# Down products of the feed-forwards: stationary split weights with 512 moving tokens, in place of stationary tokens with 128 moving columns

## The chip, the cores and the metric

The kernel runs on one core of one Trainium2 chip. The metric is the device time of one execution in microseconds. The kernel before took 3348.98 us (median of three runs, 3345.56 to 3355.31).

## The reference

4096 tokens (8 chunks of 512) of width 128 go through six stages, each preceded by a layer norm and added back to x: a gated mixture of experts (F0a), a banded attention (A0), the same mixture again (F0b), a second mixture (F1a), an attention by hyperbolic distance (A1), and that second mixture again (F1b). Only the four feed-forwards are changed. What they compute:

```python
# F0a, F0b: two shared and eight routed feed-forwards, hidden width 256
_ffn = silu(x @ w1.T) * (x @ w3.T) @ w2.T
x = x + 0.5 * (sum over e of cw[t, e] * _ffn_e(norm(x)) + sum of the two shared ones)
# F1a, F1b: eight routed ones, hidden width 512; cw is 0 where an expert's capacity is passed
h = square(relu(norm(x) @ c_fc[e]))
x = x + 0.5 * sum over e of cw[t, e] * (h @ c_proj[e])
```

cw holds two non-zero weights for each token (a softmax over its two best logits). Both kernels compute every expert for every token and weigh the results.

## The kernel before, in words

Tokens are handled in chunks of 512. XT holds the normed tokens transposed (128 features on the partitions, tokens along the row), X the running sum with tokens on the partitions. Each feed-forward phase (ffn_phase) first runs the routing (route_vector and its partners) as a program block of its own and then, after all engines have met, a loop over the 8 chunks.

The up products use float32r operands, split into a high part and a rest: xs holds the chunk's tokens as hi and lo (split_gpsimd, L199 and L201), up_hi and up_lo the weights. For each block j of 128 hidden units (20 of them in F0, 32 in F1) TensorE makes w_lo*x_hi + w_hi*x_lo + w_hi*x_hi (L221 to L223), each with 128x128 stationary weights and 512 moving tokens; in F0 a block has two such groups, w1 and w3. ScalarE takes Silu or Relu out of PSUM (L257), VectorE multiplies by the w3 product or by itself (L282). The down products (L231) are plain float32: the stationary side is 128 tokens of hT, the moving side 128 columns of dn, so that each hidden block costs four products, and each product is two instructions in the trace. They lie one expert behind the up products. VectorE then multiplies each expert's output by its routing weight and adds it up (L290), four instructions of 128x128 per expert, the last of them into X. While chunk c runs, the norm of chunk c-1 is worked in at fixed experts e (stats at 0, apply at 2, turn at 3, logits at 5 and 6). In F1 the up weights are loaded at the start of the phase and split by ScalarE (L658) and GpSimd (L644).

Order is fixed by the code of each engine and by semaphores; nothing is scheduled automatically. Banks: four for the up products in rotation, two for the down products.

Of the kernel before, what the change touches and what calls it, by code (L numbers as in the profile page):

```python
# [13 lines left out]
P = 128  # L14
# [5 lines left out]
E = 8  # L20
# [14 lines left out]
def macaron(nc, x, alpha, w_qkv0, bias_rows0, wo0, wo0_t, wfc0, router0, expert_bias, up0, down0,  # L35
            w_qkv1, wo1, router1, up1, down1, out, stop_after=99):
    ctx = ExitStack()
    with ctx:
# [21 lines left out]
        cw = sb("cw", [P, TILES, E])  # L60
        cw_c = sb("cw_c", [P, TPC, E])
# [12 lines left out]
        staged_free = sem("staged_free")  # L74
# [7 lines left out]
        for n in names:  # L82
            kinds = ["tr_done", "xt_copied", "lg_done", "lg_copied", "var_ready", "rstd_ready", "xn_ready"]
            if n == "P":
                kinds.append("split_done")
            if n[0] == "F":
                kinds += ["xs_free", "split_done", "up_done", "act_done", "h_ready", "dn_done", "acc_done"]
# [114 lines left out]

        def ffn_tensor(eng, s, lay, XS, hT, w_hi, w_lo, dn, nxt):
            U, HB, G, RING = ffn_shape(lay)
            free = s["h_ready"] if lay == 0 else s["act_done"]
            norm_credits_tensor(eng, s)
            eng.sem_inc(s["dn_done"], 2)
            eng.sem_inc(s["xs_free"], 2)
            with eng.Fori(0, B) as c:
                eng.wait_ge(s["split_done"], c + 1)  # L210
                xh = XS[:, bass.ds((c % 2) * 2 * S, S)]
                xl = XS[:, bass.ds((c % 2) * 2 * S + S, S)]
                for e in range(U + 1):
                    if e < U:
                        for hb in range(HB):
                            j = e * HB + hb
                            eng.wait_ge(free, c * (U * HB) + j + 1)
                            for g in range(G):
                                bank = (j * G + g) % 4
                                cols = slice((hb * G + g) * P, (hb * G + g + 1) * P)  # L220
                                eng.matmul(ps[:, bank, :], w_lo[:, e, cols], xh, start=True, stop=False)  # L221
                                eng.matmul(ps[:, bank, :], w_hi[:, e, cols], xl, start=False, stop=False)  # L222
                                last = eng.matmul(ps[:, bank, :], w_hi[:, e, cols], xh, start=False, stop=True)  # L223
                            last.then_inc(s["up_done"], 1)
                    if e > 0:
# [1588 lines left out]
```

## Time and profile before

| | |
|---|---|
| median of 3 runs | 3348.98 us |
| profiled execution | 3349.0 us, span 3347.2 us |
| mean granted TensorE clock | 0.861 of full speed |
| F0a, first up product to last accumulation | 63.5 to 435.7 us |
| F0b | 965.2 to 1344.8 us |
| F1a | 1380.1 to 1790.5 us |
| F1b | 2933.4 to 3339.9 us |

Busy shares over the whole span are TensorE 83%, VectorE 67%, ScalarE 56%, GpSimd 26%. They mix stages that differ: in the four feed-forwards TensorE is busy nearly all the time at the full clock, in A1 (1791 to 2925 us) the granted clock is 0.67. So the stages are read one by one: busy times by stretch, then the timeline of one engine inside a stretch, then the list of who waited for whom.

### The profile page before, as it was taken

What the parts mean: (1) busy time and instruction counts of PE and PEld (TensorE: products, weight loads), DVE (VectorE), ACT (ScalarE), POOL (GpSimd) and SP (SyncE); (2) the same over time, 40 slices, a digit from 0 to 9 for tenths busy, and PEclk for the clock granted to TensorE, in tenths of its full rate; (3) what the DMA queues carried; (4) which work ended last, traced back from release to release, by engine and by line L of the source; (5) the groups of instructions that cost most, each with busy time, mean ns of one, the idle gap of its engine ahead of it and who ended that gap; (6) DMA issues with size and microseconds to landing.
All of it is one profiled execution on the core that took longest, in us unless ns stands there. A gap on an engine that the chain in (4) does not pass through costs nothing. (4 is left out here: it accounts for less than half of the span.)

```text
span 3347.2 us, 52294 instructions
## 1 busy us (share of the span) xinstructions
PE 2792.1 (83%) x17860; PEld 2081.7 (62%) x17862; DVE 2227.0 (67%) x5046; ACT 1886.0 (56%) x2052; POOL 875.3 (26%) x584
## 2 busy tenths in 40 slices
PE   4999968888869999699996687787787787399998
PEld 4888856666658888599995232332232332189998
DVE  5555557777745555666666787787877878456665
ACT  2222237677712222334431999999999999433333
POOL 1000010000000000100001657666766767300000
PEclk9999979999979999799997667667666766699999
DMA  2000000000000000100000000000000000100000
GB/s 82 0 0 0 0 1 2 0 0 0 0 1 0 0 0 0 51 0 0 0 0 0 0 0 0 1 1 1 1 1 0 0 0 0 50 1 0 0 0 25
DMA packets 3224, 18.43 MB, mean 6 GB/s; under 512 B 1088, under 2 KB 2112, under 8 KB 2112
## 3 DMA queue, kind: packets, MB, share of 16 engines
q1 hardware_dynamic: 3136, 17.32, 1.3%
q8 instruction: 48, 0.79, 0.1%
q14 instruction: 40, 0.33, 0.0%
HBM read 15.22 MB, written 2.10 MB: 5 GB/s over the span
## 5 line engine op out<-in xcount | busy, mean ns | idle before, releaser
L1402 POOL TENSOR_TENSOR A_Y<-A_Y,A_U 128x2048 f32<-128x2048 f32 x86 | 389.8, 4554 | 227.7 <-ACT A_U L1445 227.7
L1478 DVE TENSOR_SCALAR A_U<-ps 128x1024 f32<-128x1024 f32 x256 | 309.2, 1218 | 125.6 <-POOL A_Y L1402 64.7
L140 POOL TENSOR_TENSOR rstd<-var_eps,half_neg 128x4 f32<-128x4 f32 x45 | 49.7, 1105 | 1208.0 <-DVE var_eps L120 1183.1
L1484 DVE SCALAR_TENSOR_TENSOR A_U<-ps,A_U 128x1024 f32<-128x1024 f32 x256 | 311.2, 1216 | 58.8 <-PE ps L1614 58.8
L1614 PE MATMUL ps<-A_QT,A_KT 9*128 9x512 f32 x512 | 182.9, 711 | 195.5 <-DVE A_U L1484 162.6
L257 ACT ACTIVATE F1b_act<-ps 128x512 f32<-128x512 f32 x256 | 153.2, 598 | 247.4 <-PE ps L223 231.2
L257 ACT ACTIVATE F1a_act<-ps 128x512 f32<-128x512 f32 x256 | 153.2, 598 | 243.2 <-PE ps L223 226.8
L1614 PEld LDWEIGHTS ps<-A_QT,A_KT 9*128 9x128 f32 x512 | 66.6, 256 | 333.7 <-DVE A_U L1484 235.8
L257 ACT ACTIVATE F0b_act<-ps 128x512 f32<-128x512 f32 x160 | 95.6, 598 | 273.5 <-PE ps L223 273.5
L257 ACT ACTIVATE F0a_act<-ps 128x512 f32<-128x512 f32 x160 | 95.6, 598 | 266.2 <-PE ps L223 266.2
L231 PEld LDWEIGHTS ps<-dn,F1b_hT 128*128 128x128 f32 x2048 | 237.2, 192 | 4.4
L231 PEld LDWEIGHTS ps<-dn,F1a_hT 128*128 128x128 f32 x2048 | 237.2, 192 | 4.4
L231 PE MATMUL ps<-dn,F1a_hT 128*128 128x128 f32 x2048 | 237.6, 275 | 0.0
L231 PE MATMUL ps<-dn,F1b_hT 128*128 128x128 f32 x2048 | 237.6, 275 | 0.0
L1445 ACT ACTIVATE A_U<-A_U 128x2048 f32<-128x2048 f32 (+1 forms) x96 | 236.5, 2464 | 0.0
L1586 PE MATMUL ps<-A_Y,A_VA 128*32 128x512 f32 x688 | 228.7, 798 | 5.8 <-DVE A_OT L1384 3.0
L841 ACT ACTIVATE A_M<-A_M,A_nmax 128x192 f32<-128x192 f32 (+1 forms) x512 | 203.9, 471 | 35.4 <-DVE A_nmax L956 34.1
L1402 POOL TENSOR_TENSOR dn<-dn,A_U 128x2048 f32<-128x2048 f32 x42 | 190.7, 4563 | 114.2 <-ACT A_U L1445 114.2
L956 DVE CUSTOM_DVE_ANT_0 A_M<-ps,A_mask 128x192 f32<-128x192 f32 (+1 forms) x512 | 169.2, 387 | 46.8 <-PE ps L1007 46.0
L1603 PE MATMUL ps<-A_QT,A_KT 28*128 28x512 f32 x512 | 168.3, 675 | 37.3 <-DVE A_U L1478 32.9
L282 DVE TENSOR_TENSOR F0b_hT<-F0b_act,ps 128x512 f32<-128x512 f32 x160 | 109.4, 688 | 119.1 <-ACT F0b_act L257 118.0
L1444 ACT ACTIVATE A_Y<-A_U 128x2048 f32<-128x2048 f32 (+1 forms) x64 | 159.3, 2489 | 50.8 <-DVE A_U L1484 50.6
(336 smaller groups left out, 6635.5 us busy)
## 6 DMA issues: line engine op xcount, KB each, us to landing
dn<-in_down SPq DMA_DIRECT2D x2, 2048.0 KB, 12.5
stage<-in_up SPq DMA_DIRECT2D x1, 2560.0 KB, 9.3
X<-in_x SPq DMA_DIRECT2D x1, 2048.0 KB, 7.9
F1a_up<-in_up SPq DMA_DIRECT2D x1, 2048.0 KB, 7.9
F1b_up<-in_up SPq DMA_DIRECT2D x1, 2048.0 KB, 8.1
out_x<-X SPq DMA_DIRECT2D x1, 2048.0 KB, 6.3
dn<-in_down SPq DMA_DIRECT2D x1, 1280.0 KB, 11.9
qkv_w_s<-in_w_qkv SPq DMA_DIRECT2D x2, 192.0 KB
```

Source lines behind the costliest of these rows:

```text
L231: last = eng.matmul(ps[:, 4 + d % 2, t * P:(t + 1) * P], hT[:, d % 2, hb, t * P:(t + 1) * P], dn[:, d, hb, :], start=(hb == 0), stop=(hb = ...
L257: eng.activation(act_out[:, j % RING, :], ps[:, (j * G) % 4, :], ACT.Silu if lay == 0 else ACT.Relu).then_inc(s["act_done"], 1)
L841: last = eng.activation(m, m, ACT.Exp, scale=-1.0, bias=nmax[:, n % MR, b, r:r + 1])
L956: last = eng.tensor_tensor_reduce(M[:, n % MR, b, r, w0:w1], ps[:, 2 * (n % 2) + b, r * WIN + w0:r * WIN + w1], mask[:, w0:w1], -1.0, 3e38 ...
L1402: eng.tensor_tensor(flat(y_slot(m, h)), flat(y_slot(m, h)), flat(Um[:, h % UR]), ALU.add).then_inc(s["t_ready"], 1)
L1444: eng.activation(y, u, ACT.Sqrt, bias=1.0)
L1445: eng.activation(u, u, ACT.Sqrt).then_inc(s["s_ready"], 2 if joined else 1)
L1478: eng.tensor_scalar(u_step(n), d_pair(n), 0.0, None, ALU.max).then_inc(s["dp_vector"], 1)
L1484: eng.scalar_tensor_tensor(out=u, in0=g_pair(), scalar=CLAMP, in1=u, op0=ALU.min, op1=ALU.mult).then_inc(s["u_ready"], 1)
L1586: last = eng.matmul(ps[j:j + 32, OUT, :], VA[:, v0:v0 + 32], y_slot(m, h)[:, kt, :], start=(kt == 0), stop=(kt == TPC - 1))
L1603: last = eng.matmul(ps[:, 2 * (n % 2) + b, :], KT[r:r + 28, pair, kt * P:(kt + 1) * P], QT[r:r + 28, pair, :], start=True, stop=True)
L1614: last = eng.matmul(ps[:, 4 + b, :], KT[r:r + 9, pair, kt * P:(kt + 1) * P], QT[r:r + 9, pair, :], start=True, stop=True)
```

## The change

The down product is turned round. The stationary side is now a 128x128 block of the down weights, split into dn_hi and dn_lo at the start of each phase (ScalarE L908, GpSimd L933), and the moving side is 512 tokens of the hidden activation, split into hi and lo (tile hl). Three float32r products per hidden block (L268 to L270) add into one PSUM bank over all blocks of all experts, so the chunk's output comes out once, transposed; ScalarE copies it out (yT), TensorE turns it back with four transposes, and VectorE adds it to X in one instruction. Since experts are now summed in PSUM, the routing weight must enter before the product. It is laid out along the row, broadcast to all partitions: the routing result cw is transposed on TensorE, copied by ScalarE (as a square root in F1, since the weighed value is squared afterwards), written to DRAM, and read back for each chunk in two halves of 1 MB (weights_sync) into cwb.

In F0 GpSimd multiplies the product of each routed block by cwb, ScalarE makes hi by a copy, VectorE makes lo by a subtraction. In F1 VectorE does relu times cwb in one instruction, ScalarE squares; for even blocks ScalarE and VectorE make hi and lo, for odd blocks GpSimd makes both, behind a small gate instruction. The block of its own for the routing is gone: the routing runs at the head of the phase's one block. The down products of block j are issued after the up products of block j+4 (F0) or j+5 (F1). The order of ScalarE's work at the start of F1 changes: both weight copies stand ahead of the routing's exponential.

```diff
-                    if e > 0:
-                        d = e - 1
-                        eng.wait_ge(s["h_ready"], c * (U * HB) + (d + 1) * HB + RING)
-                        eng.wait_ge(s["acc_done"], c * U + d + 1)
-                        for t in range(TPC):
-                            for hb in range(HB):
-                                last = eng.matmul(ps[:, 4 + d % 2, t * P:(t + 1) * P],
-                                                  hT[:, d % 2, hb, t * P:(t + 1) * P], dn[:, d, hb, :],
-                                                  start=(hb == 0), stop=(hb == HB - 1))
+                y, hi, lo = ps[:, 4 + p, :], hl[:, 0, j % slots, :], hl[:, 1, j % slots, :]
+                eng.matmul(y, dn_lo[:, e, hb, :], hi, start=(j == 0), stop=False)
+                eng.matmul(y, dn_hi[:, e, hb, :], lo, start=False, stop=False)
+                eng.matmul(y, dn_hi[:, e, hb, :], hi, start=False, stop=(j == N - 1)).then_inc(s["down_done"], 1)
...
+            def turn_back(c, p):
+                eng.wait_ge(s["y_copied"], c)
+                for t in range(TPC):
+                    last = eng.transpose(ps[:, 4 + p, t * P:(t + 1) * P], yT[:, t * P:(t + 1) * P], ident[:, :])
+                last.then_inc(s["y_back"], 1)
...
+        def gated_vector(eng, s, h, hl, nxt):
+            def rest(c, j):
+                eng.wait_ge(s["hi_done"], c * N + j + 1)
+                eng.tensor_tensor(hl[:, 1, j % slots, :], h[:, j % ring, :], hl[:, 0, j % slots, :].bitcast(F32),
+                                  ALU.subtract).then_inc(s["lo_done"], 1)
+            def chunk(c, p, done):
+                for j in range(N):
+                    z = h[:, j % ring, :]
+                    eng.wait_ge(s["pre_done"], c * N + j + 1)
+                    eng.tensor_tensor(z, z, ps[:, (j * G + 1) % 4, :], ALU.mult).then_inc(s["prod_done"], 1)
+                    if j >= 2:
+                        rest(c, j - 2)
...
+        def squared_vector(eng, s, h, hl, cwb, loads, nxt):
+                    eng.wait_ge(s["up_done"], n + 1)
+                    eng.scalar_tensor_tensor(out=h[:, j % ring, :], in0=ps[:, j % 4, :], scalar=0.0,
+                                             in1=cwb[:, j // HB, :], op0=ALU.max, op1=ALU.mult).then_inc(s["pre_done"], 1)
+                    if j >= 2:
+                        if not on_pool(j - 2):
+                            rest(c, j - 2)
...
+        def gated_gpsimd(eng, s, XS, h, cwb, loads, nxt):
+                    eng.wait_ge(s["prod_done"], c * N + j + 1)
+                    eng.tensor_tensor(z, z, cwb[:, r // HB, :], ALU.mult).then_inc(s["weighed"], 1)
...
+        def squared_gpsimd(eng, s, XS, h, hl, nxt):
+                split_gpsimd(eng, s, XS, (c + 1) % B, 1 - p)
+                for j in range(N):
+                    if not on_pool(j):
+                        continue
+                    eng.wait_ge(s["sq_done"], n + 1)
+                    gate_gpsimd(eng)
+                    eng.tensor_copy(hi, z)
+                    eng.drain()
+                    eng.tensor_tensor(lo, z, hi.bitcast(F32), ALU.subtract).then_inc(s["lo_pool"], 1)
...
+        def weights_sync(eng, s, lay, cw_t, cwb, turned, n):
+            eng.wait_ge(step, turned)
+            eng.dma_start(rows_view, cw_t[:, :, :]).then_inc(weights_out, 16)
+            eng.wait_ge(weights_out, 16 * (n + 1))
+            for c in range(B):
+                for half in range(2):
+                    if c > 0:
+                        eng.wait_ge(used, (c - 1) * each + (half + 1) * each // 2)
+                    eng.dma_start(cwb[:, half * (E // 2):(half + 1) * (E // 2), :].rearrange("p e q -> p (e q)"),
+                                  rows[2 * c + half:2 * c + half + 1, :].to_broadcast([P, E // 2 * S]))\
+                        .then_inc(weights_in[half], 16)
...
                     def _(eng):
+                        if lay == 1:
+                            eng.wait_ge(load["up1"], 16 * load_number)
+                            eng.activation(w_top, w_raw, ACT.Copy).then_inc(up1_top, 1)
+                            eng.wait_ge(load["dn1"], 16 * load_number)
+                        eng.activation(dn_hi[:, :, :, :], dn_raw[:, :, :, :], ACT.Copy).then_inc(dn_top, 1)
+                        route_scalar(eng, buf, n0)
+                        keep_weights_scalar(eng, cw_t, m0, lay)
```

TensorE in the first chunk of F0a, where ps is PSUM and hT the hidden activation. Before, after an expert's up products come the eight down products of the expert ahead of it:

```order
L222 MATMUL ps<-F0a_xs,up_hi 128x512
L223 MATMUL ps<-F0a_xs,up_hi 128x512
L228 ISA
L231 MATMUL ps<-dn,F0a_hT 128x128 x8
L217 REGISTER_ALU
L221 MATMUL ps<-F0a_xs,up_lo 128x512
```

The same place in the changed kernel, where hl is the split activation:

```order
L252 MATMUL ps<-F0a_xs,up_hi 128x512
L253 MATMUL ps<-F0a_xs,up_hi 128x512
L268 MATMUL ps<-F0a_hl,F0a_dn_lo 128x512
L269 MATMUL ps<-F0a_hl,F0a_dn_hi 128x512
L270 MATMUL ps<-F0a_hl,F0a_dn_hi 128x512
L251 MATMUL ps<-F0a_xs,up_lo 128x512
```

Eight short products per expert have become three long ones per hidden block, six per expert in F0, spread evenly between the up products.

GpSimd from the start of F1a on, with the semaphores waited for. Before, it has the split of the up weights, the splits of the tokens and the root of the norm:

```order
L644 TENSOR_TENSOR up_lo<-F1a_up,up_hi 128x4096 [waits up1_top]
L412 UNCONDITIONAL_BRANCH
L689 UNCONDITIONAL_BRANCH [waits barrier_Pool_Activation_PE_DVE_SP_gather]
L199 CAST F1a_xs<-XT 128x512 [waits F1a_xs_free]
L201 TENSOR_TENSOR F1a_xs<-XT,F1a_xs 128x512
```

In the changed kernel:

```order
L930 TENSOR_TENSOR up_lo<-F1a_h,up_hi 128x4096 [waits up1_top]
L230 CAST F1a_xs<-XT 128x512
L232 TENSOR_TENSOR F1a_xs<-XT,F1a_xs 128x512
L933 TENSOR_TENSOR F1a_dn_lo<-dn,F1a_dn_hi 128x4096 [waits dn_top]
L230 CAST F1a_xs<-XT 128x512
L232 TENSOR_TENSOR F1a_xs<-XT,F1a_xs 128x512
L513 TENSOR_TENSOR gated<-half_neg 128x1 [waits F1a_sq_done]
L502 CAST F1a_hl<-F1a_h 128x512
L504 TENSOR_TENSOR F1a_hl<-F1a_h,F1a_hl 128x512
L513 TENSOR_TENSOR gated<-half_neg 128x1 [waits F1a_sq_done]
L502 CAST F1a_hl<-F1a_h 128x512
```

A second subtraction of 128x4096 and, for every odd block, a gate, a copy and a subtraction have been added to GpSimd's queue.

ScalarE at the start of F1a. Before, the exponential of the routing (F1a_r_ex) stands ahead of the weight copy:

```order
L388 ACTIVATE F1a_r_ex<-F1a_r_ex 128x32 [waits route_step]
L658 ACTIVATE up_hi<-F1a_up 128x4096 [waits load_up1]
```

In the changed kernel, where the routing's buffers lie in cwb:

```order
L906 ACTIVATE up_hi<-F1a_h 128x4096 [waits load_up1]
L908 ACTIVATE F1a_dn_hi<-dn 128x4096 [waits load_dn1]
L605 ACT_TABLE_LOAD
L605 ACTIVATE F1a_cwb<-F1a_cwb 128x32 [waits route_step]
L626 ACT_TABLE_LOAD
L626 ACTIVATE F1a_cw_t<-ps 128x256 [waits route_step]
```

The exponential now stands behind both copies, and so behind both loads.

## Rows read from the trace of the kernel before

**Rows 1.** Span, then busy us of PE, PEld, DVE, ACT, POOL; PEclk; DMA.
```profile
63.00:436.00 373.00, 370.72 (x2272) 327.98 (x2272) 216.81 (x592) 103.43 (x176) 23.08 (x25) 1.00 0.00 0
...
1380.00:1791.00 411.00, 409.33 (x2848) 377.72 (x2848) 265.70 (x625) 161.00 (x272) 30.29 (x24) 1.00 0.00 0
```

**Rows 2.** Waits inside F0a, 100 to 400 us: total us, times, longest.
```profile
PEld ps L221 <- DVE F0a_hT L282: 3.3, 7, 0.5
```

**Rows 3.** Timeline of F0a, TensorE: start us, duration us, line, operation.
```profile
199.97 0.39 PE L221 MATMUL ps<-F0a_xs,up_lo 128*128 x1
...
200.65 3.73 PE L231 MATMUL ps<-dn,F0a_hT 128*128 128x128 f32 x32
...
204.14 0.48 PE L221 MATMUL ps<-F0a_xs,up_lo 128*128 x1
```

**Rows 4.** One line's instructions, L221: count, ns min/median/max, first and last start.
```profile
L221 PE MATMUL ps<-F0a_xs,up_lo x320: 389/390/790, 63.5 to 430.1; 128*128 x160
...
L221 PE MATMUL ps<-F1a_xs,up_lo x256: 388/389/790, 1380.1 to 1781.4; 128*128 x128
...
L221 PE MATMUL ps<-F1b_xs,up_lo x256: 389/389/792, 2933.4 to 3330.8; 128*128 x128
```

**Rows 5.** The same view, L290, the last accumulation of each chunk, four a chunk.
```profile
L290 DVE SCALAR_TENSOR_TENSOR X<-ps,cw_c,F0a_acc x32: 339/341/351, 112.3 to 435.4; 128x128 f32 x32
...
L290 DVE SCALAR_TENSOR_TENSOR X<-ps,cw_c,F1a_acc x32: 339/342/351, 1433.1 to 1790.2; 128x128 f32 x32
...
L290 DVE SCALAR_TENSOR_TENSOR X<-ps,cw_c,F1b_acc x32: 339/342/351, 2985.8 to 3339.6; 128x128 f32 x32
```

**Rows 6.** The same view, ScalarE's L257 and VectorE's L282.
```profile
L257 ACT ACTIVATE F0a_act<-ps x160: 597/598/600, 66.4 to 431.0; 128x512 f32<-128x512 f32 x160
...
L282 DVE TENSOR_TENSOR F1a_hT<-F1a_act x256: 676/692/1096, 1382.4 to 1782.9; 128x512 f32<-128x512 f32 x128
```

**Rows 7.** The same view, GpSimd's copy L199 and subtraction L201.
```profile
L199 POOL CAST F0a_xs<-XT x9: 609/610/611, 61.1 to 395.5; - x8, 128x512 fp32r<-128x512 f32 x1
...
L201 POOL TENSOR_TENSOR F0a_xs<-XT,F0a_xs x9: 1260/1292/1302, 61.9 to 396.3; - x8, 128x512 fp32r<-128x512 f32 x1
```

**Rows 8.** Timeline at 1817 us, GpSimd's gate and the copy behind it.
```profile
1817.53 0.19 POOL L1212 TENSOR_TENSOR A_gated<-half_neg 128x1 f32<-128x1 f32 x1 [0.18 <-issue]
1817.85 0.61 POOL L1219 COPY A_xa<-XT 128x512 f32<-128x512 f32 x1
```

**Rows 9.** Timeline at 1439 us, VectorE and GpSimd side by side in F1a.
```profile
1438.98 2.91 DVE L282 TENSOR_TENSOR F1a_hT<-F1a_act 128x512 f32<-128x512 f32 x4
...
1440.49 0.85 POOL L199 CAST F1a_xs<-XT  x1
1441.57 1.47 POOL L201 TENSOR_TENSOR F1a_xs<-XT,F1a_xs  x1 [0.23 <-issue]
```

**Rows 10.** Timeline of the start of F1a.
```profile
1360.80 0.23 ACT L388 ACTIVATE F1a_r_ex<-F1a_r_ex 128x32 f32<-128x32 f32 x1 [5.79 <-DVEq L346]
...
1361.61 3.62 ACT L658 ACTIVATE up_hi<-F1a_up 128x4096 fp32r<-128x4096 f32 x1 [0.58 <-DMA F1a_up<-in_up]
...
1365.31 8.81 POOL L644 TENSOR_TENSOR up_lo<-F1a_up,up_hi 128x4096 fp32r<-128x4096 f32 x1 [17.78 <-ACT up_hi L658]
...
1366.58 8.15 DVE L374 SCALAR_TENSOR_TENSOR F1a_r_oh<-F1a_r_rank,F1a_r_oh 128x256 f32<-128x256 f32 x2
...
1376.14 0.29 DVE L383 TENSOR_SCALAR cw<-F1a_r_work 128x256 f32<-128x256 f32 x1
```

**Rows 11.** DMA issues: count, KB each, median us from issue to landing.
```profile
dn<-in_down SPq DMA_DIRECT2D x2, 2048.0 KB, 12.5
...
X<-in_x SPq DMA_DIRECT2D x1, 2048.0 KB, 7.9
```

**Rows 12.** Timeline of the start of F0a, the routing's last step.
```profile
59.77 0.29 DVE L383 TENSOR_SCALAR cw<-F0a_r_work 128x256 f32<-128x256 f32 x1
```

**Rows 13.** Timeline of the end of F0b.
```profile
1344.86 0.88 DVE L115 BATCH_NORM_STATS2 bn<-X 128x6 f32<-128x128 f32 x4
```

More of the change, by code:

```diff
@@ L83, in macaron @@
             kinds = ["tr_done", "xt_copied", "lg_done", "lg_copied", "var_ready", "rstd_ready", "xn_ready"]
+            if n == "F1b":
+                kinds = []
+            if n in ("P", "F0a", "F1a"):
+                kinds = [k for k in kinds if k != "lg_copied" and (k != "lg_done" or n == "P")]
             if n == "P":
@@ L98, in macaron @@
         ENGINES = 4
+        LAG, RING, SLOTS = (4, 5), (5, 8), (4, 8)
+        PART = 2
+        AT = ({"y_copy": 4, "turn_back": 6, "add": 7, "root": 8, "apply": 9, "turn": 11, "copy": 12, "score": 14},
+              {"y_copy": 5, "turn_back": 8, "add": 9, "root": 11, "apply": 13, "turn": 16, "copy": 18, "score": 20})
         def barrier(eng, k):
@@ L266, in ffn_vector @@
+        def gated_vector(eng, s, h, hl, nxt):
+            U, HB, G = ffn_shape(0)
+            N, slots, ring, at = U * HB, SLOTS[0], RING[0], AT[0]
             if nxt != "end":
                 norm_credits_vector(eng, s, nxt)
[L268 to L302 removed]
@@ new lines, in chunk @@
+            def chunk(c, p, done):
+                for j in range(N):
+                    z = h[:, j % ring, :]
+                    eng.wait_ge(s["pre_done"], c * N + j + 1)
+                    eng.tensor_tensor(z, z, ps[:, (j * G + 1) % 4, :], ALU.mult).then_inc(s["prod_done"], 1)
+                    if j >= 2:
+                        rest(c, j - 2)
+                    elif done:
+                        rest(c - 1, N + j - 2)
+                    if done:
+                        between_vector(eng, s, c, p, j, at, nxt)
@@ new lines, in gated_gpsimd, with chunk @@
+        def gated_gpsimd(eng, s, XS, h, cwb, loads, nxt):
+            U, HB, G = ffn_shape(0)
+            N, ring, at = U * HB, RING[0], AT[0]
+            def chunk(c, p, done):
+                if done:
+                    eng.wait_ge(s["up_done"], c * N)
+                split_gpsimd(eng, s, XS, (c + 1) % B, 1 - p)
+                for j in range(NSH * HB, N):
+                    r = j - NSH * HB
+                    z = h[:, j % ring, :]
+                    if r % (E * HB // 2) == 0:
+                        eng.wait_ge(weights_in[2 * r // (E * HB)], 16 * (loads + c + 1))
+                    eng.wait_ge(s["prod_done"], c * N + j + 1)
+                    eng.tensor_tensor(z, z, cwb[:, r // HB, :], ALU.mult).then_inc(s["weighed"], 1)
+                    if done and nxt != "end" and j == at["root"]:
+                        norm_gpsimd(eng, s, c - 1)
+            all_chunks(eng, chunk)
+            if nxt != "end":
+                norm_gpsimd(eng, s, B - 1)
```

443 lines of the change are left out of this document (284 added, 159 removed).

## The prediction

> **What bounds the kernel now.** I read busy time by stretch first. In F0a TensorE is busy 370.7 of 373 us, in F1a 409.3 of 411, both at the full clock (2.4 GHz) [rows 1]; VectorE has 217 and 266 us, ScalarE 103 and 161, GpSimd 23 and 30. The waits say the same: over 300 us of F0a TensorE waited 3.3 us [rows 2]. So a feed-forward phase lasts as long as TensorE's products, and each chunk takes 46.0 us in F0a ((435.4 - 0.8 - 112.3)/7, the 0.8 taking the last start back by three instructions), 50.9 in F1a and 50.4 in F1b [rows 5]. From the first up product to the end of the last accumulation that is 372.2, 410.4 and 406.5 us [rows 4, 5]. F0b has the pattern of F0a.
>
> **The gain on TensorE.** Three up products start at 199.97, and the down products at 200.65: 0.227 us for each 512-column product. The 32 down instructions take from 200.65 to 204.14: 0.109 us each [rows 3]. A hidden block now costs four products of two instructions, 8 x 0.109 = 0.872 us; in the changed kernel three products of the up kind, 3 x 0.227 = 0.681. F0 has 20 blocks a chunk, F1 32, so the products alone take 180 x 0.227 = 40.9 us (F0) and 192 x 0.227 = 43.6 (F1). Add four transposes for the output and four for the norm, each at 0.116 by the nearest kind of instruction (0.109 here, and I allow for their waits): 0.9. I add 0.5 in F0 for one hold-up a chunk, explained below. TensorE needs 42.3 us in F0 and 44.5 in F1. That would give back 3.7 us a chunk in F0 and about 6 in F1. A moving operand of other data at the same shape cannot well take another time; I give this term no range of its own.
>
> **Can the other engines keep up in F0?** One block may take 40.9/20 = 2.05 us. ScalarE: Silu 0.60, copy about 0.60 [rows 6]: 1.2. VectorE: the product and the rest, 0.69 each [rows 6]: 1.4, plus about 4.5 us a chunk for norm and adding (stats 0.88 [rows 13], the other pieces of like size). GpSimd: one subtraction of this shape takes 1.29 [rows 7], and the new multiplication has that shape. Here a resource counts that busy times don't show. In F1a a VectorE instruction with two operands from SBUF, two of which take 0.8 us elsewhere, took 8.15 us: it began at 1366.58 while GpSimd's 8.81 us subtraction ran from 1365.31, and its pair ended at 1374.7, just behind it [rows 10]. Against short instructions the price is smaller: beside four VectorE products that took 2.91 us in place of 2.73, GpSimd's copy took 0.85 and its subtraction 1.47, where 0.61 and 1.26 to 1.29 are usual [rows 7, 9]. I read this as: the two engines exclude each other only while the operands stream, about 0.53 of VectorE's 0.69 and 1.15 of GpSimd's 1.29. VectorE's rest and GpSimd's multiplication are both released by the same product; VectorE has its instruction next in line and comes first. GpSimd's block is then 0.55 + 1.29 = 1.85, below 2.05: it holds. The norm's statistics and the adding come between two products on VectorE (about 2.3 us together against 1.3 us of slack before TensorE runs out of PSUM banks); that and the apply are my 0.5 us. So F0 stays bound by TensorE: 8 x (46.0 - 42.3) = 30 us less per phase.
>
> The Trainium skill has a rule on this, in SBUF — State Buffer, section "SBUF: two separate sides": VectorE and GpSimd share a port pair under an exclusive lock; whichever starts first holds it for the whole instruction and the other fully blocks. The 8.15 us agrees with it; the rows at 1439 us agree less, for they show more overlap than whole instructions would allow. Its consequence for F1 is rival B below.
>
> **F1 is where it is decided.** A pair of blocks may take 2 x 43.6/32 = 2.73 us on TensorE. GpSimd has the odd block: gate to copy 0.33 start to start [rows 8] (I take 0.35), copy and the drain behind it 0.61 + 0.23 = 0.84 [rows 7, 9], subtraction 1.26, of which 0.05 overlaps the next: 2.40. VectorE has one rest per pair that collides with one of these. If it meets the subtraction, VectorE waits and takes the port when it ends, so the next gate is late by about 0.4; at the copy or in a gap it costs 0.2 to 0.4. I take 0.33, which makes 2.73. Below is 2.40 (never collides), above 2.40 + 0.69 = 3.09 (the whole instruction each time). Each chunk adds the split of the next chunk's tokens (0.61 + 0.23 + 1.26 and a collision, 2.4) and, in F1a, the root of the norm, 1.1. GpSimd: 16 x 2.73 + 3.5 = 47.2, and 0.3 for its waits: 47.5 in F1a, 46.3 in F1b. VectorE has per pair two relus at 0.69 (nearest: the same shape, [rows 6]), one rest, about 0.27 of waiting for the port and 4.5/16 of norm and adding: 2.62, nearly as much. So GpSimd, at 26% busy over the kernel now, becomes the bound of F1: 47.5 in place of TensorE's 44.5.
>
> **The starts.** F1a. The exponential now stands behind both copies on ScalarE. It ran at 1360.80; the up weights arrive at 1361.6 and their copy takes 3.6 [rows 10]; the down weights land 12.5 us after their issue at 1354.1 [rows 11], about 1366.6; their copy ends at 1370.2, the exponential after a table load at 1371.8. Eleven microseconds late, and TensorE's ranking product and VectorE's remaining routing (7.6 us when undisturbed) wait for it. GpSimd has the subtraction until 1374.1, the token split until 1376.3, and then the second 8.8 us subtraction until 1385; VectorE's two-operand instructions stand still in both [rows 10]. Routing ends near 1390.5 (1376.4 before). Then transposes and copy 0.8, the write to DRAM, and the broadcast: 2 MB land in 7.9 us [rows 11], so I take 5 for 1 MB (bounds 2 and 8) and 2.3 for the small write. The first relu is at about 1399 in place of 1381.8: 17.5 us later. Bounds: 9 less if VectorE gets through beside the second subtraction, 3 more if both halves of the broadcast must land. F1b the same. F0: the subtraction of 128x2560 is 2560/4096 x 8.8 = 5.5 us on GpSimd and holds up the routing, which ends at 60.1 [rows 12], by as much; its own block and the token split that followed it, 3.4 us up to 63.5 [rows 4], fall away, and transposes, the halving in the preamble and the drains take 1.7. Net 3.8 later. The broadcast is hidden there, since the first four blocks of a chunk need no weights.
>
> **The ends.** Behind the last up product the chain is now, in F0, Silu, product, multiplication, copy, rest, down product, copy, transposes and adding, about 7.3 us, against 4.7 before; part is covered by the down products still to be done. I take +3.2 per F0 phase, and for F1 5 us beyond 8 chunks (filling and this tail). Later broadcasts are released half a chunk (22 us) ahead: hidden. SyncE has nothing queued behind them that anyone wants earlier.
>
> **Sum.** F0: -30 + 3.2 + 3.8 = -23 each, -46. F1a: 8 x 47.5 + 5 + 17.5 - 410.4 = -7.9. F1b: 8 x 46.3 + 22.5 - 406.5 = -13.6. Together -67.5. The profiled execution took 3349.0 (span 3347.2 and 1.8 around it), which is the median; 3349.0 - 67.5 = 3281.5 us.
>
> **The rivals.**
> (A) The port costs nothing that matters, and TensorE bounds F1 too: 44.5 x 8 + 22.5 gives -31.9 and -28.0; with -46 that is -106: 3243. For it: 2.40 without collisions is under 2.73. Against: the stretched rows [rows 9], and that GpSimd's chunk extras leave only 44.5 - 3.5 = 41.0 for 16 pairs, 2.56 each.
> (B) The slower side: in F1 every rest takes its full 0.69 out of GpSimd's pair. 16 x 3.09 + 3.9 = 53.3 a chunk in F1a, 52.2 in F1b: +38 and +34, with -46 it is +26: 3375. It decides from a mean chunk of 51.1 us on, a pair of 2.98. For it: [rows 10]. Against: [rows 9], where the two overlap. This is also where the skill's rule, taken to the letter, would lead.
> (C) The order at the port turns round in F0: GpSimd first, VectorE's rest waits 1.2 us and its next product with it, 2.6 us a block. A chunk is 16 x 2.6 + 4 x 2.05 + 2 = 51.8: +46 + 7 per phase, +106 - 21.5 = +85: 3433. Against: VectorE's next instruction is always nearer than a semaphore's release, about 0.1 us; for it, that this is thin.
> (D) The hold-ups lower TensorE's clock. The feed-forwards run at 1.00 with TensorE 99% busy; it would be some 93% here. Half the clock would cost over 100 us a phase; I see no reason for more than traces of it.
>
> **How the numbers follow.** Forecast 0.47, A 0.22, B 0.19, C 0.07, D and others 0.05. The forecast's own range is 3255 to 3310 (starts 9 less or 3 more in each F1, a pair 0.1 us either way, 13 a phase). A difference under 0.3%, 10 us, cannot be told from none. Faster: the forecast, A, and the part of B near its turning point, 0.76; same 0.05; slower 0.19. The range takes in A and B: 3238 to 3375.
>
> **What would show it.** Right: chunks of 42 to 43 us in F0 with TensorE hardly waiting; 46 to 49 in F1 with TensorE waiting for GpSimd's L504 and GpSimd above 90% busy; L431 and L504 longer than 0.69 and 1.26; the exponential of F1a after both copies and the routing chain standing still beside L933; first relu 17 us later. Wrong: L268 to L270 more than 0.23 us apart; TensorE waiting for VectorE in F0; a granted clock under 0.95 in a feed-forward; GpSimd with idle time in F1.

## The result and the profile after

The changed kernel takes 3321.64 us (median of 4 runs, 3316.97 to 3324.87) beside 3351.7 for the kernel before on the same chip: a ratio of 0.9911, 95% interval 0.989 to 0.9932. It is faster, by 30 us where 67.5 were forecast. The profiled execution took 3321.05 us, its span 3319.3, which is 27.9 less than before. By stretch, from rows of the two traces:

| | before | after | difference | forecast |
|---|---|---|---|---|
| F0a, first up product to last accumulation | 372.2 | 352.0 | -20.2 | -26.8 |
| F0a, start (first up product) | 63.5 | 67.7 | +4.2 | +3.8 |
| F0b, phase and start | | | -20.7 + 3.7 | -26.8 + 3.8 |
| F1a, weight loads issued to first relu | 28.1 | 45.8 | +17.7 | +17.5 |
| F1a, first relu to last accumulation | 408.7 | 405.9 | -2.8 | -25.4 |
| F1b, weight loads issued to last accumulation | 433.2 | 420.1 | -13.1 | -13.6 |
| A0 and A1 | | | +4.9, -2.6 | 0 |

These add to -28.9; the remaining +1.0 lies in seams between them. The attentions are not changed. A0, whose code is the same in all traces of the changed kernel and its variants, took from 498 to 508 us in them (from F0a's last accumulation to A0's last write of X; 499 before), so the stages are compared one by one.

Busy time by stretch, to be read against [rows 1] (columns: span, then busy us of PE, PEld, DVE, ACT, POOL; PEclk; DMA share, GB/s); the last two are six chunks each, of F1a and of F1b. What has changed most is the last busy column, GpSimd's, 247 us in F0a for 23:

```profile
63.00:436.00 373.00, 343.51 (x1508) 277.89 (x1508) 252.59 (x451) 195.35 (x351) 247.34 (x155) 0.98 0.12 46
...
1429.00:1736.00 307.00, 281.37 (x1203) 222.81 (x1202) 264.24 (x373) 184.20 (x307) 251.62 (x307) 0.97 0.12 41
2996.00:3273.00 277.00, 270.91 (x1178) 221.66 (x1177) 231.16 (x295) 183.74 (x294) 247.73 (x302) 0.98 0.12 46
```

TensorE is busy 98% of the time in F1b and 92% in F1a, GpSimd 89% and 82%. The accumulations into X (L380, one a chunk), which answer to [rows 5], give the time of a chunk:

```profile
L380 DVE TENSOR_TENSOR X<-X,ps x7: 680/681/682, 126.2 to 387.3; 128x512 f32 x6, 128x512 f32<-128x512 f32 x1
...
L380 DVE TENSOR_TENSOR X<-X,ps x7: 676/677/679, 1429.4 to 1736.1; 128x512 f32 x6, 128x512 f32<-128x512 f32 x1
L380 DVE TENSOR_TENSOR X<-X,ps x7: 671/677/679, 2996.2 to 3273.5; 128x512 f32 x6, 128x512 f32<-128x512 f32 x1
```

A sixth of each distance is 43.5 us in F0a (46.0 before), 51.1 in F1a (50.9) and 46.2 in F1b (50.4). F0b has 44.5. Beside forecasts of 42.3, 47.5 and 46.3, it is F1a that is furthest off. F1a and F1b run the same code but for one thing: F1b is the last stage and prepares no norm.

The waits in F1a, 1420 to 1760 us (total us, times, longest), to be read against [rows 2]:

```profile
POOL gated L513 <- ACT F1a_h L359: 29.8, 14, 2.7
...
PEld ps L268 <- POOL F1a_hl L504: 24.3, 44, 2.6
DVE xn L141 <- POOL rstd L155: 18.9, 7, 2.9
...
PE ps L161 <- DVE xn L141: 15.0, 7, 2.5
PE ps L268 <- POOL F1a_hl L504: 14.2, 7, 2.2
```

Two things hold TensorE up: seven times the norm (L161 transposes what L141 has normed), and GpSimd's split of the odd blocks (L504). One such norm in the timeline, VectorE, ScalarE and GpSimd around 1640 us:

```profile
1636.27 1.04 DVE L135 TENSOR_SCALAR var_eps<-mv 128x4 f32<-128x4 f32 x1
...
1640.22 0.68 DVE L445 SCALAR_TENSOR_TENSOR F1a_h<-ps,F1a_cwb 128x512 f32<-128x512 f32 x1
...
1641.23 1.30 POOL L504 TENSOR_TENSOR F1a_hl<-F1a_h,F1a_hl 128x512 fp32r<-128x512 f32 x1
...
1642.49 1.01 POOL L155 TENSOR_TENSOR rstd<-var_eps,half_neg 128x4 f32<-128x4 f32 x1
...
1643.53 2.41 DVE L141 TENSOR_SCALAR xn<-X,mv,rstd 128x128 f32 x4 [2.63 <-POOL rstd L155]
...
1645.86 0.68 DVE L445 SCALAR_TENSOR_TENSOR F1a_h<-ps,F1a_cwb 128x512 f32<-128x512 f32 x1
1646.06 0.42 PEld L161 LDWEIGHTS ps<-ident,xn 128*128 128x128 f32 x4 [2.79 <-issue]
1646.07 0.66 PE L161 MATMUL ps<-ident,xn 128*128 128x128 f32 x4 [2.37 <-DVE xn L141]
...
1646.57 0.63 ACT L359 ACTIVATE F1a_h<-F1a_h 128x512 f32<-128x512 f32 x1 [4.96 <-DVE F1a_h L445]
```

The variance is there at 1637.3, but GpSimd's root stands in its program behind the block whose subtraction ends at 1642.5. GpSimd was not busy when the variance came: it stood idle for 2.60 us until 1639.89, waiting for that block's square, and so it did in four of the seven norms. It is the place of the root in GpSimd's order that delays it. VectorE has come to the apply by 1640.9 and waits 2.63 us for a root of 1.01; then the apply takes 2.41 beside GpSimd's copy and subtraction (one of its four instructions has a median of 0.34 over the whole kernel). No relu starts between 1640.9 and 1645.9. TensorE stops for 2.4 us, ScalarE for 5.0, and the first odd block after it comes late to GpSimd (gate, 2.67 us idle at 1648.53).

The clock has a part in F1 too. After some of its stops TensorE is granted the lower of its two clock levels (1.2 GHz) for some products; such a row is called a low-clock stretch below. Two such stretches, one in F1a and one in F1b (columns as above, clock 0.50), and TensorE at the first of them:

```profile
1628.00:1631.00 3.00, 3.00 (x8) 2.33 (x8) 0.69 (x1) 0.63 (x1) 2.58 (x5) 0.50 0.00 0
3130.00:3133.00 3.00, 3.00 (x9) 2.33 (x8) 0.70 (x2) 0.24 (x1) 2.59 (x5) 0.50 0.00 0
```

```profile
1627.01 0.50 PE L268 MATMUL ps<-F1a_hl,F1a_dn_lo 128*128 128x512 f32 x1 [2.21 <-POOL F1a_hl L504]
...
1628.19 0.63 PE L252 MATMUL ps<-F1a_xs,up_hi 128*128 128x512 f32 x1
1628.62 0.63 PE L253 MATMUL ps<-F1a_xs,up_hi 128*128 128x512 f32 x1
```

The products stand 0.43 us apart in place of 0.227. There are five low-clock stretches of about eight products in the six chunks of F1a and three in those of F1b; before the change there was none in the same chunks. Each begins within 2 us of a stop of TensorE of 1.9 to 2.4 us (of the fifteen stops of over 1 us in the two windows, seven are not followed by one). The chunks of F1b alternate by it: 47.4 to 48.2 us with a stop and a low-clock stretch, 44.75 without either; 46.2 is their mean.

The start of F1a, to be read against [rows 10]:

```profile
1326.03 0.33 SPq L888 DMA_DIRECT2D F1a_h<-in_up  x1
...
1337.47 8.83 POOL L930 TENSOR_TENSOR up_lo<-F1a_h,up_hi 128x4096 fp32r<-128x4096 f32 x1 [18.02 <-ACT up_hi L906]
1338.66 3.62 ACT L908 ACTIVATE F1a_dn_hi<-dn 128x4096 fp32r<-128x4096 f32 x1 [1.26 <-DMA dn<-in_down]
...
1343.59 0.23 ACT L605 ACTIVATE F1a_cwb<-F1a_cwb 128x32 f32<-128x32 f32 x1
...
1347.93 11.74 DVE L577 TENSOR_TENSOR_SCAN F1a_cwb<-ones_f,F1a_cwb 128x64 f32<-128x64 f32 x8
1348.21 8.80 POOL L933 TENSOR_TENSOR F1a_dn_lo<-dn,F1a_dn_hi 128x4096 fp32r<-128x4096 f32 x1
...
1371.84 1.29 DVE L445 SCALAR_TENSOR_TENSOR F1a_h<-ps,F1a_cwb 128x512 f32<-128x512 f32 x2 [7.61 <-DMA F1a_cwb<-weight_rows]
```

The exponential stands behind both copies, 17.6 us after the loads were issued (7.1 before), and VectorE's eight scans, the running sums of the routing, stand still beside L933.

### The profile page after: what moved, and what is told of

It is laid out like the page before. It is cut to its first block and busy times, and to the rows that moved or that the text cites. A ratio compares the mean times of both kernels' runs of the same rounds, so it can differ in the third digit from the quotient of the medians.

```text
span 3319.3 us, 44950 instructions
## 1 busy us (share of the span) xinstructions
PE 2659.7 (80%) x13816; PEld 1821.9 (55%) x13818; DVE 2459.2 (74%) x4431; ACT 2246.8 (68%) x2661; POOL 1954.8 (59%) x1609
## 5 line engine op out<-in xcount | busy, mean ns | idle before, releaser
L477 POOL TENSOR_TENSOR F0b_h<-F0b_h,dn 128x512 f32<-128x512 f32 x128 | 212.4, 1663 | 123.2 <-DVE F0b_h L408 123.0
L477 POOL TENSOR_TENSOR F0a_h<-F0a_h,dn 128x512 f32<-128x512 f32 x128 | 212.6, 1666 | 116.0 <-DVE F0a_h L408 115.8
L359 ACT ACTIVATE F1a_h<-F1a_h 128x512 f32<-128x512 f32 x256 | 157.6, 630 | 149.5 <-DVE F1a_h L445 149.1
L359 ACT ACTIVATE F1b_h<-F1b_h 128x512 f32<-128x512 f32 x256 | 160.3, 632 | 118.2 <-DVE F1b_h L445 116.6
L1040 POOL TENSOR_TENSOR A_VA<-A_v_new,bv 128x384 f32<-128x384 f32 (+1 forms) x16 | 13.6, 868 | 375.7 <-PE ps L1279 362.6
L445 DVE SCALAR_TENSOR_TENSOR F1b_h<-ps,F1b_cwb 128x512 f32<-128x512 f32 x256 | 171.5, 684 | 60.3 <-PE ps L253 48.1
L330 ACT ACTIVATE F0b_h<-ps 128x512 f32<-128x512 f32 x160 | 95.8, 598 | 161.6 <-PE ps L253 161.6
L1203 DVE CUSTOM_DVE_ANT_0 A_M<-ps,A_mask 128x192 f32<-128x192 f32 (+1 forms) x512 | 169.3, 387 | 47.1 <-PE ps L1254 46.2
L1849 PE MATMUL ps<-A_QT,A_KT 28*128 28x512 f32 x512 | 167.7, 672 | 42.3 <-DVE A_U L1724 38.1
L330 ACT ACTIVATE F0a_h<-ps 128x512 f32<-128x512 f32 x160 | 95.7, 598 | 154.6 <-PE ps L253 154.6
L445 DVE SCALAR_TENSOR_TENSOR F1a_h<-ps,F1a_cwb 128x512 f32<-128x512 f32 x256 | 167.4, 680 | 37.9 <-PE ps L253 29.7
L408 DVE TENSOR_TENSOR F0b_h<-F0b_h,ps 128x512 f32<-128x512 f32 x160 | 109.8, 686 | 102.9 <-ACT F0b_h L330 102.3
```

The lines of the kernel that those rows point to most:

```text
L330: eng.activation(h[:, j % ring, :], ps[:, (j * G) % 4, :], ACT.Silu).then_inc(s["pre_done"], 1)
L359: eng.activation(z, z, ACT.Square).then_inc(s["sq_done"], 1)
L445: eng.scalar_tensor_tensor(out=h[:, j % ring, :], in0=ps[:, j % 4, :], scalar=0.0, in1=cwb[:, j // HB, :], op0=ALU.max, op1=ALU.mult).then ...
L477: eng.tensor_tensor(z, z, cwb[:, r // HB, :], ALU.mult).then_inc(s["weighed"], 1)
L1203: last = eng.tensor_tensor_reduce(M[:, n % MR, b, r, w0:w1], ps[:, 2 * (n % 2) + b, r * WIN + w0:r * WIN + w1], mask[:, w0:w1], -1.0, 3e38 ...
```

## The experiments

The theories tested: (1) F1a's surplus comes from the place of the norm: its apply stands too soon behind the root asked of GpSimd; against it (2) the SBUF port shared by VectorE and GpSimd takes it all. A third question is the start. All edits are made to the changed kernel; AT holds, for F0 and F1, the block at which each piece of the norm is worked in.

**e1_norm_later_f1**: in F1 the apply and what follows it four blocks later, nothing else.

```diff
-  ... "root": 11, "apply": 13, "turn": 16, "copy": 18, "score": 20})
+  ... "root": 11, "apply": 17, "turn": 20, "copy": 22, "score": 24})
```

> The changed kernel with one edit: in F1 the norm of the chunk before is applied at block 17 in place of 13, turned at 20 (16), copied at 22 (18). Nothing else moves. Theory N (the norm chain is the surplus of F1a: VectorE stands at the apply waiting for GpSimd's root, which is queued behind GpSimd's own backlog, and TensorE stands at the turn): the seven waits of the apply on the root (18.9 us in 1420 to 1760) and of the turn on the apply (15.0) nearly vanish, chunks of F1a fall from 51.1 to about 47, the span from 3319 to about 3287. Rival P (GpSimd's total work plus the shared port is the surplus, wherever the norm stands): chunks of F1a stay within 50 to 51.5 and the time within 5 us of the changed kernel's. F1b has no norm and stays at 46.2 in both.

Measured: 3296.61 us (4 runs, 3290.13 to 3300.95), ratio to before 0.9842 (0.9824 to 0.986), 25 us less than the changed kernel. Its accumulations, and VectorE around a norm in F1a:

```profile
L380 DVE TENSOR_TENSOR X<-X,ps x7: 677/678/679, 1423.1 to 1708.8; 128x512 f32 x6, 128x512 f32<-128x512 f32 x1
```

```profile
1623.76 0.69 DVE L445 SCALAR_TENSOR_TENSOR F1a_h<-ps,F1a_cwb 128x512 f32<-128x512 f32 x1
1624.37 2.45 DVE L141 TENSOR_SCALAR xn<-X,mv,rstd 128x128 f32 x4
1626.73 0.68 DVE L445 SCALAR_TENSOR_TENSOR F1a_h<-ps,F1a_cwb 128x512 f32<-128x512 f32 x1
```

A chunk of F1a takes 47.6 us in place of 51.1, and the phase from the first relu on is 23.1 us shorter (382.8 for 405.9); F1b stays at 46.25, F0 at 43.5. The apply is as long as before (2.45), but no longer waits, and the waits of L141 and L161 inside the phase are gone. TensorE still stops once a chunk for L504, 1.7 to 2.0 us, but the five low-clock stretches are gone. So 3.5 of the 4.9 us by which an F1a chunk exceeded one of F1b came from the place of the norm's steps; in them is what the lower clock cost, at most 1.3 us by estimate (five times eight products at 0.2 us more, over six chunks). The 1.4 us left are near the 1.2 that the forecast gave the norm's root on GpSimd. Whether an earlier root would do as well as a later apply was not tried.

**e2_norm_later_f0**: the same in F0 (apply 9 to 11, turn 11 to 13, copy 12 to 14, score 14 to 16), one run.

> The changed kernel with one edit: in F0 the norm is applied at block 11 in place of 9, turned at 13 (11), copied at 14 (12), scored at 16 (14). Theory N: the 0.9 us of VectorE's wait for the root and the 1.0 us of TensorE's wait at the turn go, chunks fall from 43.5 to about 42.6 in F0a and from 44.45 to 43.5 in F0b. Rival (VectorE's surplus work, not its wait, holds TensorE up, whichever block it stands at): chunks stay within 0.2 us of 43.5 and 44.45.

Measured: 3311.27 us, 10 less than the changed kernel's median, whose own runs lie 8 us apart, so that it is the chunks that decide: 42.8 us in F0a and 43.7 in F0b, 0.73 and 0.75 less, F1 unchanged. The wait of TensorE for the normed tokens, from 100 to 400 us, in the changed kernel and in this one:

```profile
PE ps L161 <- DVE xn L141: 6.8, 7, 1.0
```

```profile
PE ps L161 <- DVE xn L141: 1.6, 7, 0.3
```

The same cause, smaller, since GpSimd has a gap between two blocks in F0. Seven chunks of a phase work in a norm, the first does not; 14 times 0.74 make 10.4 us, and the two phases are 4.7 and 5.7 us shorter.

**e3_routing_first**: the order at the start. In F1 ScalarE's exponential stands ahead of both copies; in all four phases GpSimd's dn_lo waits until the routing is done, and TensorE waits for the split down weights only before its first down product.

```diff
                         if lay == 1:
+                            route_scalar(eng, buf, n0)
                             eng.wait_ge(load["up1"], 16 * load_number)
...
                             eng.activation(dn_hi[:, :, :, :], dn_raw[:, :, :, :], ACT.Copy).then_inc(dn_top, 1)
-                        route_scalar(eng, buf, n0)
... on GpSimd, ahead of dn_lo:
+                        eng.wait_ge(step, m0 + 1)
... on TensorE, from the head of the phase to its first down product:
-                        eng.wait_ge(dn_split, number + 1)
+                if j == 0 and done == 0:
+                    eng.wait_ge(dn_split, ...)
```

> The changed kernel with the starts reordered: in F1 the routing's exponential stands ahead of both weight copies on ScalarE; in all four phases GpSimd's split of the down weights waits until the routing is done, and TensorE waits for it only before the first down product. Theory L (late exponential plus VectorE standing still beside GpSimd's long subtractions makes the late start): the first relu of F1a comes 10 to 14 us earlier than in the changed kernel, counted from the issue of the phase's loads (45.8 us there), the starts of F0 come 4 to 5 us earlier; together about 30 us, 3290. Rival W (the routing weights' way through DRAM makes it): the interval from load issue to first relu shrinks by less than 4 us in F1, and the time by less than 12.

Measured: 3285.78 us (4 runs, 3278.42 to 3289.36), ratio 0.9809 (0.9792 to 0.9825), 36 less than the changed kernel. The start of F1a in its trace:

```profile
1309.72 0.33 SPq L890 DMA_DIRECT2D F1a_h<-in_up  x1
...
1316.70 0.23 ACT L607 ACTIVATE F1a_cwb<-F1a_cwb 128x32 f32<-128x32 f32 x1 [5.70 <-DVEq L563]
...
1318.89 1.57 DVE L579 TENSOR_TENSOR_SCAN F1a_cwb<-ones_f,F1a_cwb 128x64 f32<-128x64 f32 x8
...
1321.20 8.84 POOL L933 TENSOR_TENSOR up_lo<-F1a_h,up_hi 128x4096 fp32r<-128x4096 f32 x1 [18.06 <-ACT up_hi L910]
...
1322.47 8.60 DVE L591 SCALAR_TENSOR_TENSOR F1a_cwb<-F1a_cwb 128x256 f32<-128x256 f32 x2
...
1341.26 1.89 DVE L447 SCALAR_TENSOR_TENSOR F1a_h<-ps,F1a_cwb 128x512 f32<-128x512 f32 x3 [7.46 <-DMA F1a_cwb<-weight_rows]
```

From the loads' issue to the first relu it is 31.6 us in place of 45.8 (28.1 before the change), in F1b 31.7 for 47.2, F0a's first Silu comes 5.9 us earlier (64.75 for 70.68), and from A0's last write of X to F0b's first up product it is 28.6 for 34.2. Together 14.3 + 15.5 + 5.9 + 5.6 = 41.3. Some of it is lost again: the split of the down weights now ends after the first relu (L937, 1333.97 + 8.90), and the phases from the first relu on are 0.7 us (F1a) and 3.2 us (F1b) longer. 37.4 us are left, beside 35.9 between the medians. F1a takes 14 us less where 10 to 14 were expected; rival W is refuted. The scans now take 1.57 us; one collision with the first subtraction is left (L591, 8.60). The later chunks stay (43.5, 44.5, 51.0, 46.5).

**e4_rest_off_port**: the rest (low part) of the even blocks in F1 reads one operand from PSUM and so only one from SBUF. This kernel computes other values in F1, and so does e6 below; the number and shape of the instructions are the same.

```diff
-                eng.tensor_tensor(hl[:, 1, j % slots, :], h[:, j % ring, :], hl[:, 0, j % slots, :].bitcast(F32),
+                eng.tensor_tensor(hl[:, 1, j % slots, :], ps[:, 7, :], h[:, j % ring, :],
```

> The changed kernel, where VectorE's subtraction for the low part in F1 (even blocks) reads PSUM bank 7 and h in place of h and hl: the same length of instruction, one operand from SBUF, so the values are others. It takes VectorE off the port that it shares with GpSimd. If the shared port sets the pair of 2.78 us: GpSimd's gate returns from 0.48 us mean to 0.2, VectorE's L431 from 1.26 to 0.69, chunks of F1b fall from 46.2 to about 44.7, which is TensorE's own 44.5. If GpSimd's work alone sets it, chunks of F1b stay at 46 or more. F1a: the norm stall stays if it comes from GpSimd's queue order (chunks of 48 or more), and goes if it came from the port (about 45).

Measured: 3274.98 us (one run); chunks of 47.7 us in F1a and 44.0 in F1b, 3.4 and 2.25 less. The two instructions that collide, in the changed kernel and then in this one (ns min/median/max):

```profile
L431 DVE TENSOR_TENSOR F1b_hl<-F1b_h,F1b_hl x128: 677/1348/1744, 2940.6 to 3304.1; 128x512 fp32r<-128x512 f32 x128
...
L513 POOL TENSOR_TENSOR gated<-half_neg x256: 183/639/661, 1374.5 to 3306.0; 128x1 f32<-128x1 f32 x128
```

```profile
L431 DVE TENSOR_TENSOR F1b_hl<-ps,F1b_h x128: 680/681/693, 2912.8 to 3258.9; 128x512 fp32r<-128x512 f32 x128
...
L513 POOL TENSOR_TENSOR gated<-half_neg x256: 185/195/212, 1374.3 to 3259.5; 128x1 f32<-128x1 f32 x128
```

The collision is real: 0.45 us at GpSimd's gate. But the norm's hold-up stays without it, 1420 to 1760 us (the eighth time is the phase's end):

```profile
PE ps L161 <- DVE xn L141: 20.0, 8, 4.7
DVE xn L141 <- POOL rstd L155: 18.3, 8, 2.7
```

Without the collision TensorE has no stop and no low-clock stretch in F1b, whose chunk is TensorE's own 44.0. So theory 2 explains all of F1b's surplus and does not explain why F1a is 3.8 us a chunk longer than F1b here too.

**e6_norm_later_off_port**: the edits of e1 and e4 together.

> The changed kernel with the norm later in F1 and VectorE's subtraction of F1 reading PSUM bank 7 (other values). If norm stall and port are the whole surplus of F1a, its chunks come to about 45 (51.1 now, 47.6 and 47.7 with one of the two), that is TensorE's 44.5. If something third is there, 46 or more.

Measured: 3261.74 us (one run). Busy time in six chunks of F1a and of F1b:

```profile
1431.00:1700.00 269.00, 268.73 (x1202) 220.53 (x1201) 213.88 (x373) 185.77 (x306) 216.48 (x307) 1.00 0.13 47
2951.00:3216.00 265.00, 265.00 (x1182) 219.49 (x1181) 194.44 (x296) 185.60 (x296) 212.87 (x301) 1.00 0.13 48
```

Chunks of 44.8 and 44.0 us with TensorE never idle. The two causes can be taken away one by one: of 51.1 us, the place of the norm has 3.5 (e1) or 2.9 (47.7 to 44.8 here), the port 3.4 or 2.8, and 44.8 is TensorE's own time. They add up but for 0.6 us, 6.3 together for 6.9 singly.

**c1_three_together**: the edits of e1, e2 and e3.

> The changed kernel with the three edits together: norm later in F1, norm later in F0, routing ahead of the weight copies. If the causes are separate they add: F0 chunks 42.8 and 43.7, F1a 47.6, F1b 46.2, first relu 31.6 us after the issue of the loads. From the changed kernel's 3321.6 by the single edits: -31 (norm in F1), -12 (norm in F0), -35 (start) = 3244. If the causes overlap (the start's gain is eaten by the norm's stall or the other way), 3255 or more.

Measured: 3252.61 us (5 runs, 3248.36 to 3255.1), ratio 0.9704 (0.9683 to 0.9724) to 3354.11 for the kernel before. It is 69.0 under the changed kernel; the three edits by themselves gave 25.0 + 10.4 + 35.9 = 71.3. This kernel and the next ran on another chip than the changed kernel, so the ratios to the kernel before are the better measure: singly they fall by 0.0069 + 0.0030 + 0.0102 = 0.0201 from 0.9911, together by 0.0207. So the gains add. The time lies between the 3244 expected for that and the 3255 set for an overlap; the 3244 took 31 us for e1 from the profiled executions, and 6 of these lie in A0.

**c2_hi_on_scalar**: c1, and ScalarE makes hi for the odd blocks too, so that GpSimd has only the gate and the subtraction.

```diff
-                    if not on_pool(j):
-                        ... eng.activation(hl[:, 0, j % slots, :], z, ACT.Copy).then_inc(s["hi_done"], 1)
+                    eng.activation(hl[:, 0, j % slots, :], z, ACT.Copy)\
+                        .then_inc(s["hi_pool"] if on_pool(j) else s["hi_done"], 1)
... on GpSimd, waiting for hi_pool in place of sq_done:
-                    eng.tensor_copy(hi, z)
-                    eng.drain()
```

> The three edits together, and in F1 ScalarE makes the high part of the odd blocks too, so that GpSimd has only the gate and the subtraction: 0.84 us less of GpSimd's pair and one instruction less at the shared port. If GpSimd's pair of 2.78 us bounds F1, chunks fall to TensorE's 44 to 45, about 2.5 us in each of 16: 3204 to 3215. Rival: ScalarE, now with four instructions of 0.63 for each pair (2.5 of 2.73 us) and its waits for its own results, becomes the bound: chunks of 47 or more, no gain over the three edits.

Measured: 3214.46 us (5 runs, 3212.61 to 3218.42), ratio 0.9593 (0.9573 to 0.9613), 38 under c1. Six chunks of F1a in c1 and in c2:

```profile
1395.00:1681.00 286.00, 272.02 (x1201) 220.58 (x1200) 267.92 (x373) 186.17 (x306) 254.99 (x306) 0.99 0.12 44
```

```profile
1391.00:1667.00 276.00, 272.10 (x1205) 219.94 (x1204) 236.39 (x374) 233.67 (x405) 171.00 (x211) 1.00 0.13 46
```

In these windows ScalarE has 47.5 us of work more, which it had free, GpSimd 84 less, and VectorE, with the same instructions, 31.5 less: its time of standing at the port. A chunk takes 45.9 us in F1a (47.7 in c1) and 44.0 in F1b (46.2), which is TensorE's own time there. The time is at the upper end of the 3204 to 3215 expected. The edit takes both a collision and 0.61 us of GpSimd's work out of each pair and does not tell which of the two counted.

## Why the prediction was right and where it failed

**The gain on TensorE: right.** L268, L269 and L270 stand 0.225 us apart (starts 1636.03, 1636.25, 1636.48 in the trace of the changed kernel; 0.227 forecast), and TensorE's own time of a chunk in F1 is 44.0 without the norm and 44.8 with it (e6), 44.5 forecast.

**F1's new bound, GpSimd and the port: right for F1b.** The chunk is 46.2 us where 46.3 was forecast, GpSimd waits 1.5 us in six chunks, and e4 takes the surplus away by taking the collision away. In the rhythm that the prediction described, VectorE's rest takes the port when GpSimd's subtraction ends and the next gate is late; a pair so takes 2.77 us in the trace of e1 (gate to gate), 2.73 forecast:

```profile
1636.39 0.64 POOL L513 TENSOR_TENSOR gated<-half_neg 128x1 f32<-128x1 f32 x1
1637.16 0.61 POOL L502 CAST F1a_hl<-F1a_h 128x512 fp32r<-128x512 f32 x1
1637.91 1.29 POOL L504 TENSOR_TENSOR F1a_hl<-F1a_h,F1a_hl 128x512 fp32r<-128x512 f32 x1
1639.16 0.65 POOL L513 TENSOR_TENSOR gated<-half_neg 128x1 f32<-128x1 f32 x1
```

Two terms are off in opposite directions. Without a collision the pair is 2.32 us and not 2.40 (from start to start, gate to copy 0.32, copy to subtraction 0.75 where 0.84 was taken, subtraction to gate 1.25), and the collision costs 0.45 here, not 0.33. Over all pairs of F1b, collided or not, the mean price is 0.37: gate 0.39, copy 0.74 and subtraction 1.35 us on average, beside 0.195, 0.61 and 1.30 in e4. And the sum has each chunk alike, where every other one has a stop and a low-clock stretch. The closeness of 46.2 to 46.3 is in part luck.

Rival B had a chunk of 51.1 as its point of decision, and F1a has 51.1, but not by its mechanism: it wants 3.09 us a pair and 52.2 in F1b. Rival A, the port for nothing, falls with the gate's 0.64 and with e4. The Trainium skill (SBUF — State Buffer, section "SBUF: two separate sides") says that the engine which comes second fully blocks. L431's 1.74 us (0.68 when free) and the 11.74 us of the scans beside L933 agree. The gate agrees as well: in the trace of e1 an L431 that began at 1635.31 ended at 1636.98, and the gate that began at 1636.39 ended 0.05 us behind it. But the second engine loses less than the whole instruction of the first, 0.45 us of 0.68 at the gate, which is why rival B's price is too high: part of the blocked instruction's own 0.19 passes beside the other.

**The starts of F1: right**, 17.7 us for 17.5 (F1b 47.2 in all), by the steps named: the exponential behind both copies, VectorE standing still beside L933, a broadcast of 1 MB landing in 4.6 us for 5. The routing ended 1.4 us later after the loads' issue than forecast (38.2 for 36.8), the way through DRAM took less. e3 shows the cause by taking it away. F0's start: +4.2 for +3.8.

**The step that failed: the norm in F1a.** "Each chunk adds ... in F1a, the root of the norm, 1.1", with VectorE's norm counted among its busy times. The sum asked only how long each engine works, and the norm is a chain that goes from VectorE to GpSimd and back to VectorE; its waiting stands in no term. With GpSimd busy 30 us in the whole phase [rows 1], a root was done as soon as its input was. Now it has a place behind an odd block, waits for that block's square, then for its gate, copy and subtraction (2.6 us), and everything behind the apply in VectorE's order stands with it: from the variance at 1637.3 to the root at 1643.5 it is 6.2 us for an instruction of 1.0. The apply, taken as a piece "of like size" to the statistics' 0.88, takes 2.41 against GpSimd. Together VectorE starts no relu for 5.0 us, more than four PSUM banks can bridge: TensorE stops for 2.4.

The chunk of 51.1 is 3.6 over the forecast, 28.9 in eight. The ends gave 8.0 back (the phase is 3.0 us shorter than eight chunks, where 5 more was forecast), for one because the first chunk works in no norm. So this term, with the ends, makes 20.9 of the 22.8 us that are missing in F1a; 1.7 is that the forecast's 410.4 counts from the first up product and the table from the first relu, 0.2 the start. e1 moved nothing but the apply and the three steps behind it and gave 25 us back, 23.1 of them in this phase.

The prediction's own signs said so: of those for wrong, "GpSimd with idle time in F1" came in F1a (29.8 us at the gate) and "TensorE waiting for VectorE in F0" came too (6.8 us in 300); of those for right, 46 to 49 us a chunk holds for F1b alone, GpSimd above 90% busy for neither (89% and 82%).

**The same step in F0, smaller.** 0.5 us was allowed for hold-ups; the chunk came out at 43.5 for 42.3, and e2 gives 0.7 of these 1.2 back; the other 0.5 stay open. The tail of F0, forecast at +3.2, cost nothing (352.0 is 8 x 43.52 + 3.8; before, 372.2 is 8 x 46.04 + 3.9). Net, 6.6 us short in F0a.

**The missing sum.** 67.5 - 27.9 = 39.6: 22.8 in F1a, 7.0 and 6.0 in F0a and F0b, 0.5 in F1b, 2.3 in the attentions, 1.0 in seams.

**The other rivals.** Rival D, the hold-ups lowering TensorE's clock, has a small part and not none: the low-clock stretches in F1 cost TensorE about 1.6 us each (eight products at 0.2 more), by this estimate 1.3 us a chunk in F1a and 0.8 in F1b, inside the surpluses that e1 and e4 take away. No run changes the clock alone, so this share stays an estimate. The granted clock was 0.97 and 0.98 in the stretches above, and in the first chunk of F1a and of F1b 0.94 (0.96 before), just under the 0.95 of the prediction's sign. Rival C, GpSimd first at the port in F0, has next to none:

```profile
L477 POOL TENSOR_TENSOR F0a_h<-F0a_h,dn x128: 1279/1685/1756, 78.4 to 413.6; 128x512 f32<-128x512 f32 x128
```

GpSimd's multiplication takes 1.69 us in the median, 1.28 at least, while VectorE's rest (L401) keeps its median of 0.685 (mean 0.76, single ones up to 1.77). So VectorE comes first and GpSimd loses 0.4 us, where the prediction took 0.55. GpSimd also waited 93 us for VectorE's product between 100 and 400 us.

Left open: the +4.9 us of A0 (e1, with the same code there, had 6 us less), the 0.5 us a chunk in F0, why some stops of TensorE are followed by a low-clock stretch and others not (in F1a of e1, none), and what GpSimd would save without its gate, which was not tried.

## What to carry to other kernels

Work given to an idle engine delays every short step that this engine does for others, even while the engine stands idle, since the step has its place in the engine's order behind work that waits for something else. List the round trips through it (who asks, at which place in the order, who waits), price each by all that stands ahead of it, waits included, and not by its own duration (6.2 us for 1.0 here), and move the use of its result as far behind its request as that takes. Two stages with the same code but for one small task are a free experiment: the difference of 4.9 us between F1a and F1b pointed at the norm before any run. Put an exponential or another small step with many followers ahead of large copies that wait for loads, not behind them.

## What the hardware showed unexpectedly

- A GpSimd instruction of one column (the gate, 0.19 us alone) takes 0.64 us when a VectorE subtraction with two SBUF operands has just taken the port, and ends 0.05 us behind it (e1); with one operand from PSUM it is 0.195 again (e4).
- VectorE's TENSOR_SCALAR with one large SBUF operand (L141, 128x128, 0.34 us each) is held up by GpSimd as well: 2.41 us for four, 2.45 in e1. So it is not only instructions with two large operands.
- Eight short scans that take 1.57 us together when free (e3) took 11.74 when they began 0.28 us ahead of GpSimd's subtraction of 8.80: they were done only 2.66 us behind its end, past the next token split's instructions too (L577).
- A stop of TensorE of about 2 us can be followed by the lower clock: after 8 of 15 stops in the windows of F1, some eight products stood 0.43 us apart in place of 0.227. Stop and low-clock stretch together make chunks of 47.4 to 48.2 us beside 44.75 in F1b.
